# Moving the 8-bit scaling of the inner activations from VectorE to ScalarE in a gated cross-attention layer

## What is computed

```python
def act_quant(x):
    scale = 127.0 / jnp.clip(jnp.max(jnp.abs(x), axis=-1, keepdims=True), 1e-05)
    q = jnp.clip(jnp.round(x * scale), -128.0, 127.0) / scale
    return x + jax.lax.stop_gradient(q - x)
def bitlinear158(x, w, b):
    xq = act_quant(rms_norm(x))
    wq = weight_quant(w)                  # to -1, 0, 1
    return jnp.einsum('bsd,od->bso', xq, wq) + b
h = jax.nn.silu(bitlinear158(x, w1, b1))           # inner width 1024
h = jax.nn.gelu(h, approximate=False)
h = layer_norm(h, ln_g, ln_b)
h = bitlinear158(h, w2, b2)
x = x + jnp.tanh(g_attn) * attention(layernorm(x), context)
x = x + jnp.tanh(g_ffn) * h                        # h of layernorm(x)
```

## Time and profile before

| | |
|---|---|
| median of 3 runs | 251.71 us (251.49 to 251.83) |
| the profiled execution: its own time | 251.6 us |
| the profiled execution: first to last instruction (span) | 249.8 us |
| PE, DVE, ACT, POOL busy, share of the span | 84%, 75%, 62%, 60% |
| granted TensorE clock, mean over the span | 0.937 |

### The profile page before, as it was taken

One profiled execution on the slowest core, in us unless ns is written; L12 is line 12 of the kernel. 1 busy time (PEld: TensorE's weight loads), 2 busy tenths in 40 slices (PEclk: granted clock), 3 DMA queues, 4 the chain that ended last, 5 costly groups with the idle time before them and its releaser, 6 DMA issues.

```text
span 249.8 us, 4518 instructions
## 1 busy us (share of the span) xinstructions
PE 210.2 (84%) x1452; PEld 167.5 (67%) x1452; DVE 187.7 (75%) x430; ACT 155.6 (62%) x455; POOL 149.7 (60%) x222
## 2 busy tenths in 40 slices
PE   1799899999999999998998999899899746834453
PEld 1677788688978877886786888678678632513231
DVE  2587556689786679988988998898899842779761
ACT  2256627737557597759559875965887593849021
POOL 0415726639776469788787878778787832062630
PEclk9999999999999999999999999999999996775557
DMA  6999994000000000000000000000000000000001
GB/s 194 286 213 184 318 385 189 0 0 3 1 3 0 3 3 0 3 0 0 24 1 0 25 0 0 4 21 0 4 22 0 3 0 21 0 0 0 24 22 31
DMA packets 11357, 12.40 MB, mean 50 GB/s; under 512 B 3936, under 2 KB 10336, under 8 KB 11104
## 3 DMA queue, kind: packets, MB, share of 16 engines
q1 hardware_dynamic: 10432, 11.44, 16.6%
q10 hardware_dynamic: 896, 0.61, 0.8%
HBM read 11.00 MB, written 1.05 MB: 48 GB/s over the span
## 4 chain that ended last, share of the span: by engine, by line
PE 45%; DVE 19%; POOL 12%; issue 11%; ACT 9%; DMA 1%; DVEq 0%; SPq 0%; POOLq 0%
PE bank_pair L805 7%; PE bank_score L883 5%; PE bank_ff L920 4%; POOL h_small L430 4%; PE bank_lat L907 4%; PE bank_swap L808 3%; DVE z L1206 3%; PE bank_prob L895 3%; DVE h L1230 3%; POOL prob_room L485 3%; DVE neg_max L1289 3%; ACT prob_room L654 3%; PE bank_ff L959 3%; PE bank_ff L939 2%; POOL qcat L408 2%
## 5 line engine op out<-in xcount | busy, mean ns | idle before, releaser
L654 ACT ACTIVATE prob_room<-bank_score,neg_max 128x128 f32<-128x128 f32 x128 | 45.3, 369 | 23.5 <-DVE neg_max L1289 23.5
L485 POOL TENSOR_TENSOR prob_room<-prob_room,rsum 128x512 f32<-128x512 f32 x32 | 33.3, 1041 | 26.0 <-DVE rsum L1297 25.8
L406 POOL TENSOR_TENSOR qcat<-qcat,turned 64x256 f32<-64x256 f32 x32 | 30.8, 963 | 11.9 <-DVE turned L1141 11.8
L883 PEld LDWEIGHTS bank_score<-kcat,qcat 128*128 128x128 f32 x256 | 33.7, 192 | 2.3
L805 PE MATMUL bank_pair<-qcT,wcat 96*128 96x128 f32 x256 | 34.0, 276 | 0.0
L883 PE MATMUL bank_score<-kcat,qcat 128*128 128x128 f32 x256 | 33.7, 275 | 0.0
L642 ACT COPY probT_room<-bank_prob 128x512 f32<-128x512 f32 x32 | 19.0, 594 | 22.4 <-PE bank_prob L895 22.4
L920 PE MATMUL bank_ff<-m_sb,latT 128*128 128x256 f32 x128 | 31.9, 395 | 0.0
L805 PEld LDWEIGHTS bank_pair<-qcT,wcat 96*128 96x128 f32 x256 | 31.1, 192 | 0.4 <-DVE wcat L1126 0.2
L408 POOL TENSOR_TENSOR qcat<-qcat,turned 64x256 f32<-64x256 f32 x32 | 29.6, 924 | 2.5
L1137 DVE TENSOR_TENSOR qcat<-bank_pair,cst 128x512 f32<-128x512 f32 x32 | 21.6, 674 | 10.5 <-PE bank_swap L808 10.5
(11 more groups left out here) (163 smaller groups left out, 436.6 us busy)
## 6 DMA issues: line engine op xcount, KB each, us to landing
wo<-in_L_xattn_W_o SPq DMA_DIRECT2D x1, 2048.0 KB, 19.5
w_sb<-in_L_ffn_w SPq DMA_DIRECT2D x2, 1024.0 KB, 9.9
out_x<-y SPq DMA_DIRECT2D x8, 128.0 KB, 1.7
wuq<-in_L_xattn_W_uq SPq DMA_DIRECT2D x1, 768.0 KB, 11.5
ctx_all<-in_ctx ACTq DMA_DIRECT2D x2, 256.0 KB, 5.0
x_all<-in_x SPq DMA_DIRECT2D x2, 256.0 KB, 4.7
cst<-in_consts SPq DMA_DIRECT2D x1, 512.0 KB, 7.0
x_all<-in_x SPq DMA_DIRECT2D x1, 512.0 KB, 8.2
```

The costliest lines, as they stand in the source:

```text
L406: nc.gpsimd.tensor_tensor(odd, odd, add_odd, ALU.add).then_inc(pair_half, 1)
L485: nc.gpsimd.tensor_tensor(p, p, rsum[:, k % 2, :].unsqueeze(2).broadcast_to([P, GROUP, kts * P]), ALU.mult).then_inc(prob_scaled, 1)
L654: last = nc.scalar.activation(prob_of(n, kts)[:, j, :], src[:, j, :], ACT.Exp, bias=neg_max[:, k % 2, j:j + 1], accum_out=esum[:, k % 2, j ...
L883: last = nc.tensor.matmul(bank[:, j * kts * P:(j + 1) * kts * P], qcat[:, k, hh // 2, hh % 2, :], kcat[:, b, hh % 2, 0:kts * P], start=Fal ...
```

## The change

DVE no longer multiplies the 128x1024 tile `h`; it ends with the reciprocal `QMUL`, which raises a new semaphore `h_inverse`. ACT gets a new function `scale_h`, one activation (Copy) over 128x1024 with the scale from `QMUL` and the bias `MAGIC`, in place, which raises `hq_ready` for PE's transposes. In `body` it stands behind the tanh of step k = 1; in `after` behind each sum of squares. `xl` is quantised as before.

```diff
+            def scale_h(c):
+                act.wait_ge(h_inverse, c + 1)
+                nc.scalar.activation(h[:, slot(c), :], h[:, slot(c), :], ACT.Copy, bias=MAGIC, scale=hs(QMUL)).then_inc(hq_ready, 1)
...
                         if k == 1 and there(f, 2):
                             tanh(f - 2)
+                        if k == 1 and there(f, 3):
+                            scale_h(f - 3)
                         if k == 2 and there(f, 3):
                             copy_h(f - 3, 0)
...
                     sum_squares(F - 3)
+                    scale_h(F - 3)
                     silu(F - 1)
                     gelu(F - 1, 1.0)
                     for r in range(2):
                         copy_h(F - 3, r)
                     sum_squares(F - 2)
+                    scale_h(F - 2)
                     for r in range(2):
                         copy_h(F - 2, r)
                     sum_squares(F - 1)
+                    scale_h(F - 1)
...
-                link(nc.vector.reciprocal(small(QMUL), small(YMAX)))
-                nc.vector.tensor_scalar(src, src, small(QMUL), MAGIC, ALU.mult, ALU.add).then_inc(ready, 1)
+                inverse = nc.vector.reciprocal(small(QMUL), small(YMAX))
+                if src is None:
+                    inverse.then_inc(ready, 1)
+                else:
+                    link(inverse)
+                    nc.vector.tensor_scalar(src, src, small(QMUL), MAGIC, ALU.mult, ALU.add).then_inc(ready, 1)
...
-                quantise(h[:, slot(c), :], hs, amax, h_floor, h_scale, c + 1, hq_ready)
+                quantise(None, hs, amax, h_floor, h_scale, c + 1, h_inverse)
```

More of the change, by code:

```diff
@@ L252, in build @@
         h_scale = sem("h_scale")
+        h_inverse = sem("h_inverse")
         h_deq_ready = sem("h_deq_ready")
```

## The result

The changed kernel takes 256.54 us (median of 4 runs, 256.35 to 258.32), the kernel before 251.77 us beside it (251.49 to 252.09): the ratio is 1.0205, with a 95% interval of 1.0158 to 1.0252. It is slower, by some 4.8 us: the interval lies clear of 1, and it leaves open whether the loss is over or under 2%. The profiled execution took 256.41 us, its span is 254.5 us, 4.7 over that of before.

The account below looks back on a forecast made before the run. The prediction took a chain of waits through DVE, ACT and PE, 22.07 us a tile, as the bound. To 251.6 it added 2.8 us in the loop (4 x 0.58 + 0.45) and 2.8 behind it: 257.2 us, range 254.2 to 259.2.

Parts of the forecast that it names:

- The scaling on ACT: The new activation of `h` takes 1.15 us, between 1.06 and 1.28, and holds ACT for 1.06.
- The wait and the stop: In a loop tile, ACT idles some 2.5 us; PE stops 1.65 us at `attn_out`, nearly swallowing its later 1.17 us wait.
- The tile, +0.58: In each of four loop tiles `down` starts 0.58 us later, so the period is 22.65 us in place of 22.07.
- PE's unbroken run: In a loop tile, PE runs without gap from the last part of `attn_out` to the second half of the transposes, 5.64 us.
- The other way, ACT's: In a loop tile, ACT's exponentials start 0.45 us later, at 153.94 in place of 153.49, and its chain keeps this.
- Tile f = 7, +0.45: In the fifth tile, without projections, PE has gaps enough and only ACT's +0.45 us remains.
- Behind the loop, +2.03, +2.40, +2.80: After the loop: tile 6's reciprocal +2.03 us, its transposes +2.40, tile 7 +2.80, with a table load in full view.
- The loop had no slack: Slack rival: another engine's wait in the loop takes up the 0.58 and only the tail pays, 254.4 us; chance 8%.
- The cascade: Rival: PE's 1.17 us wait doesn't absorb the stop at `attn_out`; each loop tile loses 1.6 us, 262.4 us; chance 5%.
- The faster case: Rival: the row maximum, not ACT, still releases the loop's exponentials; each of five tiles gains up to 0.67, 248.2 us; 3%.
- The clock case: Rival: 2.4 GHz granted to PE behind the loop, from 210 to 215 us, halves those 5.00 us: 254.7 us; chance 9%.
- The drain: Rival: the newly visible table load behind the loop also stops ACT for about 1.38 us, 258.6 us; chance 3%.

Follow-up runs that it names:

- gap filled: Changed kernel plus 20 products of the unit matrix ahead of PE's wait in the last tile of the loop: 256.45 us, ratio 1.0198 against the kernel before.
- loop part alone: Against the changed kernel, ACT scales only tiles 0 to 4 and DVE again tiles 5 to 7: 254.12 us.
- silu first: Against the changed kernel, the scaling of tile 5 behind the loop stands behind the silu of tile 7, ahead of its gelu: 254.88 us.
- between the copies: Against the changed kernel, the loop's scaling stands between step 2's copies of `latT` and of the probabilities in ACT's list: 255.22 us.
- behind both copies: Against the changed kernel, the loop's scaling stands behind step 2's copies of `latT` and the probabilities, ahead of its exponentials; with no other move: 251.85 us.
- both moved: Against the changed kernel, scaling behind both copies of step 2 in the loop and, behind the loop, behind the silu of tile 7: 249.30 us.
- DVE behind the loop: Against the changed kernel, ACT scales behind both copies of step 2 in the loop, and DVE scales behind the loop: 248.96 us.

## Why the prediction was right

The forecast was 257.2 us, in 254.2 to 259.2; 256.54 was measured. Its mechanism is what the traces show, and most terms of the sum can be read off:

- *The scaling on ACT*, 1.15 us from the square and the row operand: 1.148.
- *The wait and the stop.* ACT idle 2.5 us, PE's stop 1.65, its 1.17 us wait swallowed: 2.50, 1.46 (`attn_out` starts 1.63 later against the reciprocal, which is how the 1.65 was reckoned), and no wait left.
- *The tile, +0.58.* Measured +0.50. The first step, from the reciprocal to `attn_out`, came out (1.66 us for 1.68). The transposes then ended 5.57 us later for 5.64, and the hand-over to `down` took the expected 0.69. So PE's unbroken run is the mis-sized term, by 0.07 of the 0.08 us; over four tiles it makes 0.3. The other way, ACT's, was +0.40 for a predicted +0.45.
- *Tile f = 7, +0.45.* This step failed. I wrote that PE has gaps enough there; its wait grew to 2.80 us instead and the clock fell, a cost that the term put at nothing. The result of tile 4 came 1.62 later; with the gap filled and the clock held, it was 0.41, about the term. Behind that result the changed execution gained 0.96, with the clock at 0.78 from 210 to 215 us where it had been 0.50 before the change, so that +0.66 was left at the next reciprocal. That this is near 0.45 is luck.
- *Behind the loop, +2.03, +2.40, +2.80.* Measured, each against the reciprocal of tile 5: +2.02, +2.41, +2.81. Running the scaling there alone cost 2.8 (254.44), and moving it behind the silu took 2.27 of it off.
- *The rivals.* The loop had no slack (22.57, and 254.12 with the loop part alone). The cascade did not come: 0.50 a tile, not 1.6; DVE's residual did wait, 1.07 us, and started 0.37 later against the reciprocal for a predicted 0.25, but DVE caught up behind it: `xl` was quantised 6.10 us behind the reciprocal, 6.18 before. The faster case named the right point, the hold of ACT behind the reciprocal: with the copies out of the way, the release-to-exponentials time fell below that of before and the sign turned. The clock case came in part, in both directions: down to 0.50 in tile f = 7, up to 0.78 from 210 to 215 us.
- *The drain* that the Trainium skill puts beside a table load (ScalarE: Activation LUTs, What ACT_TABLE_LOAD costs) is not in the traces: the load at 229.34 ends at 230.62, the silu starts at 230.63. The term for it was rightly left out.

The sum of the predicted terms was 5.6, and the two profiled executions are 4.8 apart: the tile's term makes -0.3, the changed execution's lead ahead of the first place of the change -0.6, tile f = 7 with what followed it +0.2, and the end behind the last transposes -0.1. The -0.6 is chance, and without it the profiled time would have been 257.0. The prediction also took 0.2% for what a measurement can tell from no change; the interval of the ratio came out at 0.5% to either side.

## What to carry to other kernels

An engine with idle time in its profile has room only behind the event that releases the new work; what stands behind that work in its list waits with it, so ask first what those instructions are and who needs them. Placed two instructions later, the same move turned from 2% slower to level, and with the end of the program left as it was, to 1.1% faster, of which the clock behind the loop gave a part (0.8 of 3.1 us between the traced executions). Work moved to another engine needs a place of its own in the steady part and at the end, since the neighbours differ: in the loop two copies, at the end a table load, a silu and a gelu.

## What the runs showed of the hardware

The granted clock where the work thins out adds to every such comparison. The stretch from the first product of f = 7 to the reciprocal of tile 5 shows it, grouped by kernels whose lists are alike up to the sum of squares of tile 5, just ahead of that reciprocal, one traced execution each:

| scaling in the loop | this stretch, us |
|---|---|
| on DVE: before; ACT for tiles 5 to 7 alone | 36.77; 36.84 |
| on ACT, ahead of both copies: changed; loop part alone; silu first | 37.43; 37.46; 37.60 |
| the same with the gap filled | 37.07 |
| on ACT, between the copies | 37.43 |
| on ACT, behind both copies: alone; both moved; DVE behind the loop | 35.45; 35.52; 35.61 |

Between the last two groups lie some 1.9 us, although their periods differ by only 0.5 us in a tile. With the scaling between the copies the clock was 0.50 from 204 to 206 us, with no stop at `attn_out` before it; behind both copies it was 1.00 there (columns as in the earlier trace rows, in this order):

```profile
204.00:206.00 2.00, 2.00 (x11) 1.33 (x10) 0.00 (x0) 1.99 (x8) 0.00 (x0) 0.50 0.00 0
```

```profile
204.00:206.00 2.00, 0.38 (x4) 0.20 (x4) 1.52 (x8) 1.57 (x7) 0.33 (x2) 1.00 0.19 66
```

The sixteen products of the last `attn_out` took from 3.69 us with the scaling between the copies to 4.74 before the change. So the order of the lists moves a total by about 1 us more than the lists themselves explain. That is why 251.85 came for 253.0 expected: against before, 1.32 us were gained in this stretch, 0.35 of them up to the result of tile 4 and 0.97 behind it. It is also why the tile period and the distances of the reciprocals, not the medians, carry the argument here.

The moment of the fall is not fixed by the list. The kernel before and the one with ACT for tiles 5 to 7 alone run the same instructions up to here, and the clock of the first was 1.00 until 208 us, that of the second 0.58 from 204 to 206. Yet executions with the same list took the same time over the stretch within 0.2 us. With two or three executions of each list that is an observation and no rule, and what sets the moment of the fall was not tested.
